# One transformer layer in split fp32 matmuls: both norms of the feed-forward input taken from one variance, and another order of work between attention and feed-forward

## The reference

```python
x = _layernorm(x + attention(x))          # (x - mean) / sqrt(var + 1e-5)
var = jnp.mean(jnp.square(x), axis=-1, keepdims=True)
nx = x * jax.lax.rsqrt(var + 1e-5) * ln_w
x = _layernorm(x + (silu(nx @ gate.T) * (nx @ up.T)) @ down.T)
```

## Time and profile before

| what | value |
|---|---|
| median of 3 runs | 1210.94 us (1209.27 to 1212.98) |
| profiled execution, own time | 1213.92 us |
| its span | 1212.1 us |
| mean granted PE clock | 0.99 |
| PE busy | 1127.9 us, 93% |
| DVE busy | 844.1 us, 70% |
| POOL busy | 780.5 us, 64% |
| ACT busy | 623.9 us, 51% |

### The profile page before, as it was taken

One profiled execution on the slowest core, in us unless ns is written; L12 is line 12 of the kernel. 1 busy time (PEld: TensorE's weight loads), 2 busy tenths in 40 slices (PEclk: granted clock), 3 DMA queues, 4 the chain that ended last, 5 costly groups with the idle time before them and its releaser, 6 DMA issues.

```text
span 1212.1 us, 18710 instructions
## 1 busy us (share of the span) xinstructions
PE 1127.9 (93%) x5346; PEld 943.9 (78%) x5346; DVE 844.1 (70%) x1451; ACT 623.9 (51%) x1138; POOL 780.5 (64%) x511
## 2 busy tenths in 40 slices
PE   7699999999999999999999999999987599999997
PEld 6587878887888788878878887888775478888886
DVE  6688788778877887888788778787888652222224
ACT  4555655555665565656655666566555352222223
POOL 3578867876896688678867886787664123334331
PEclk9999999999999999999999999999999799999999
DMA  6755555555565556565555555555555111111101
GB/s 188 211 136 147 131 135 144 152 133 134 144 159 131 146 144 152 130 153 148 142 136 134 145 136 139 143 143 128 133 134 131 64 53 52 52 52 52 35 17 70
DMA packets 148346, 148.75 MB, mean 123 GB/s; under 512 B 15200, under 2 KB 128864, under 8 KB 148320
## 3 DMA queue, kind: packets, MB, share of 16 engines
q1 hardware_dynamic: 148320, 148.43, 47.8%
HBM read 37.23 MB, written 2.10 MB: 32 GB/s over the span
## 4 chain that ended last, share of the span: by engine, by line
PE 55%; POOL 16%; DVE 13%; issue 9%; ACT 3%; DMA 2%; SPq 1%; DVEq 0%; POOLq 0%; ACTq 0%
PE ACC L1058 11%; PE ACC L1060 11%; PE ACC L1059 11%; POOL rope_s L478 5%; PE S L1058 4%; PE S L1059 4%; PE S L1060 4%; DVE PT_lo L817 4%; POOL qk_raw L481 3%; PE S L1076 3%; PE S L1074 3%; PE S L1075 3%; POOL qk_raw L477 3%; DVE y L869 3%; DVE turned L810 2%
## 5 line engine op out<-in xcount | busy, mean ns | idle before, releaser
L592 ACT ACTIVATE probs<-S,neg_max 128x128 f32<-128x128 f32 (+7 forms) x256 | 189.3, 739 | 276.6 <-DVE neg_max L799 276.6
L799 DVE CUSTOM_DVE_ANT_0 S<-S,mask 128x128 f32<-128x128 f32 (+7 forms) x256 | 194.3, 759 | 152.8 <-PE S L1076 152.3
L810 DVE STREAM_TRANSPOSE turned<-probs 128x128 f32<-128x128 f32 (+7 forms) x256 | 197.8, 773 | 8.3 <-ACT probs L592 8.3
L502 POOL TENSOR_TENSOR PT_lo<-PT_lo,PT_hi 128x512 fp32r<-128x512 f32 x64 | 118.3, 1848 | 123.1 <-ACT PT_hi L599 123.1
L869 DVE SCALAR_TENSOR_TENSOR y<-ACC,row_rcp,y 128x512 f32<-128x512 f32 x256 | 178.4, 735 | 17.1 <-PE ACC L1060 17.0
L599 ACT ACTIVATE PT_hi<-PT_lo 128x1024 fp32r<-128x1024 f32 (+3 forms) x160 | 164.8, 1030 | 12.7 <-DMA PT_lo<-turned 12.3
L1058 PE MATMUL ACC<-PT_hi,V_hi 128*128 128x512 f32 (+3 forms) x384 | 136.4, 355 | 35.2 <-DVE PT_lo L817 20.5
L817 DVE TENSOR_TENSOR PT_lo<-PT_lo,PT_hi 128x1536 fp32r<-128x1536 f32 (+2 forms) x96 | 158.7, 1654 | 4.1 <-ACT PT_hi L599 4.1
L478 POOL TENSOR_TENSOR rope_s<-rope_s,sin_sb 128x512 f32<-128x512 f32 x76 | 146.1, 1922 | 0.0
L481 POOL TENSOR_TENSOR qk_raw<-qk_raw,rope_s 128x512 f32<-128x512 f32 x76 | 134.0, 1763 | 6.0
L1074 PE MATMUL S<-K_hi,Q_hi 128*128 (+5 forms) x384 | 132.0, 344 | 4.6 <-ACT probs L592 3.8
(11 more groups left out here) (130 smaller groups left out, 2589.3 us busy)
## 6 DMA issues: line engine op xcount, KB each, us to landing
PT_lo<-turned SPq DMA_DIRECT2D x256, 128.0 KB, 2.6
PT_lo<-turned SPq DMA_DIRECT2D x128, 208.0 KB, 3.7
rope_s<-qk_raw SPq DMA_DIRECT2D x160, 128.0 KB, 2.8
PT_lo<-turned SPq DMA_DIRECT2D x128, 112.0 KB, 2.5
PT_lo<-turned SPq DMA_DIRECT2D x128, 96.0 KB, 2.4
wq_raw<-in_L_attn_wq_dram SPq DMA_DIRECT2D x32, 256.0 KB, 2.9
wkvo_raw<-in_L_attn_wo_dram SPq DMA_DIRECT2D x32, 256.0 KB, 2.7
turned<-in_L_ffn_gate_w_t_dram SPq DMA_DIRECT2D x7, 512.0 KB, 3.9
```

Of the source, the lines that this page charges most:

```text
L592: nc.scalar.activation(dst, src, ACT.Exp, bias=neg_max[:, at:at + 1], scale=-1.0, accum_out=row_sum[:, j % 2, i:i + 1]).then_inc(exp_done, 1)
L799: nc.vector.tensor_tensor_reduce(src, src, bias, scale=1.0, scalar=MASKED, op0=ALU.add, op1=ALU.min, accum_out=neg_max[:, at:at + 1]).then ...
L810: nc.vector.transpose(dst.rearrange("p b (r i) -> p r b i", i=QB), src.rearrange("p (r b i) -> p r b i", b=4, i=QB)).then_inc(turn_done, 1)
```

## The change

1. **Norms.** The RMS norm's divisor is computed from the layer norm's variance: sqrt(v (1 + 1e-5) + 1e-10), beside sqrt(v + 1e-5). `deviations` makes both with two small square roots, one DVE reciprocal inverts both (128x2x4), and `both_norm` makes `nx` from the un-normalised `y` with one subtraction and multiplication. The eight squares, their row sums and the second turn of square root and reciprocal are gone. `layer_norm` of the residual stays, and now comes after `both_norm`.
2. **Statistics.** `add_with_statistics` puts each `bn_stats` behind the next tile's addition.
3. **Low parts.** For the last head the low parts of pieces 2 and 3 are made by POOL; DVE keeps piece 4. On POOL the first gate and up low parts follow them.
4. **Order.** PE makes `transpose_rows(0)` right after pv of half 1, ahead of `rows` of tiles 4 to 7. On ACT the high parts of the gate and up weights move ahead of the high parts of pieces 3 and 4. On DVE `xT_low(0)` moves ahead of additions 6 and 7.

```diff
-                deviation(cols, mean_var[:, cols, 1], eps_ln, 1.0)
...
-            def rms_deviation(half):
-                for t in range(half * HT, (half + 1) * HT):
-                    act_e.wait_ge(ln_done, t + 1)
-                    if t >= 2:
-                        act_e.wait_ge(sq_done, t - 1)
-                    nc.scalar.activation(V_stage[:, t % 2 * HID:(t % 2 + 1) * HID], y[:, t, :], ACT.Square,
-                                         accum_out=sum_sq[:, t:t + 1]).then_inc(sq_done, 1)
-                act_e.wait_ge(sq_done, (half + 1) * HT)
-                cols = slice(half * HT, (half + 1) * HT)
-                deviation(cols, sum_sq[:, cols], eps_rms, 1.0 / HID)
+                deviation(0, cols, mean_var[:, cols, 1], eps_ln, 1.0)
+                deviation(1, cols, mean_var[:, cols, 1], eps_rms, 1.0 + RMS_EPS)
...
+            n.add("pt1", 3 * (HEADS - 1) - n["pt1"])
+            for k in (2, 3):
+                pt_low(k)
             weight_low(0, gate_raw, gT)
             weight_low(1, up_raw, uT)
...
+            weight_high(0, 0)
+            weight_high(0, 1)
             pt_high(3, HEADS - 1)
             pt_high(4, HEADS - 1)
-            layer_deviation(0)
+            deviations(0)
             split_high("pv", 1)
-            rms_deviation(0)
-            weight_high(0, 0)
-            weight_high(0, 1)
             act_e.wait_ge(ln_w_in, 16)
             xT_high(0, 0, xbank[0], scale=True)
-            layer_deviation(1)
-            rms_deviation(1)
+            deviations(1)
...
+            def add_with_statistics(ts):
+
+                for t in ts:
+                    add_rows(t, REP - 1)
+                    if t > ts[0]:
+                        statistics(t - 1, n["y"] - 1)
+                statistics(ts[-1], n["y"])
+
             splits(*LAST_STEPS[-1], last=True)
+            add_with_statistics(tiles[0])
+            for t in tiles[0]:
+                aggregate(t)
+            n.add("pt1", 2)
+            pt_low(4)
+            inverses(0)
+            for t in tiles[0]:
+                both_norm(t)
+            split_low("pv", 1, REP - 1)
+            for t in tiles[0]:
+                layer_norm(t).then_inc(ln_done, 1)
+            add_with_statistics((4, 5))
             dve.wait_ge(ln_w_in, 16)
...
+            xT_low(0)
+            add_with_statistics((6, 7))
...
             other("pv", 1, REP - 1, 0, NT)
+            transpose_rows(0)
             for t in range(HT, NT):
                 rows(t)
             y_base = n["y"]
-            transpose_rows(0)
```

More of the change, by code:

```diff
@@ L700, in _, with deviation, deviations @@
                 step(j, i, 0, last=True)
-            def deviation(cols, squares, eps, scale):
-                nc.scalar.activation(spread[:, cols], squares, ACT.Sqrt, bias=eps[:], scale=scale).then_inc(std_done, 1)
-            def layer_deviation(half):
+            def deviation(row, cols, squares, eps, scale):
+                nc.scalar.activation(spread[:, row, cols], squares, ACT.Sqrt, bias=eps[:], scale=scale).then_inc(std_done, 1)
+            def deviations(half):
                 act_e.wait_ge(var_done, (half + 1) * HT)
                 cols = slice(half * HT, (half + 1) * HT)
-                deviation(cols, mean_var[:, cols, 1], eps_ln, 1.0)
-            def rms_deviation(half):
-                for t in range(half * HT, (half + 1) * HT):
-                    act_e.wait_ge(ln_done, t + 1)
-                    if t >= 2:
-                        act_e.wait_ge(sq_done, t - 1)
-                    nc.scalar.activation(V_stage[:, t % 2 * HID:(t % 2 + 1) * HID], y[:, t, :], ACT.Square,
-                                         accum_out=sum_sq[:, t:t + 1]).then_inc(sq_done, 1)
-                act_e.wait_ge(sq_done, (half + 1) * HT)
-                cols = slice(half * HT, (half + 1) * HT)
-                deviation(cols, sum_sq[:, cols], eps_rms, 1.0 / HID)
+                deviation(0, cols, mean_var[:, cols, 1], eps_ln, 1.0)
+                deviation(1, cols, mean_var[:, cols, 1], eps_rms, 1.0 + RMS_EPS)
             def weight_high(p, which):
@@ L946, in aggregate, with inverses, norm, both_norm @@
                 nc.vector.bn_aggr(mean_var[:, t, :], stats[:, t, :]).then_inc(var_done, 1)
[L948 to L957, removed]
+            def inverses(half):
+                cols = slice(half * HT, (half + 1) * HT)
+                dve.wait_ge(std_done, 2 * half + 2)
+                nc.vector.reciprocal(inv_spread[:, :, cols], spread[:, :, cols]).then_inc(inv_done, 1)
+                dve.wait_ge(inv_done, half + 1)
+            def norm(dst, t, row):
+                return nc.vector.tensor_scalar(dst, y[:, t, :], mean_var[:, t, 0:1], inv_spread[:, row, t:t + 1],
+                                               ALU.subtract, ALU.mult)
             def layer_norm(t):
[L960 to L965, removed]
+                return norm(y[:, t, :], t, 0)
+            def both_norm(t):
+                norm(nx[t], t, 1).then_inc(nx_done, 1)
             def xT_low(half):
@@ L976, in _ @@
             tiles = [range(HT), range(HT, NT)]
-            cols = [slice(0, HT), slice(HT, NT)]
-            splits(*LAST_STEPS[-1], last=True)
-            dve.wait_ge(ln_w_in, 16)
[L980 to L996, removed]
-            y_base = n["y"]
-            xT_low(0)
-            variances(tiles[1], y_base)
-            inverses(3, cols[1])
+            def add_with_statistics(ts):
[4 more added lines that the diff above has]
+                statistics(ts[-1], n["y"])
+            splits(*LAST_STEPS[-1], last=True)
+            add_with_statistics(tiles[0])
[10 more added lines that the diff above has]
+            add_with_statistics((4, 5))
+            dve.wait_ge(ln_w_in, 16)
+            xT_low(0)
+            add_with_statistics((6, 7))
+            y_base = n["y"]
+            for t in tiles[1]:
+                aggregate(t)
+            inverses(1)
+            for t in tiles[1]:
+                both_norm(t)
             for t in tiles[1]:
                 layer_norm(t).then_inc(ln_done, 1)
-            inverses(4, cols[1])
-            for t in tiles[1]:
-                rms_norm(t)
             product(0, 0, first=True)
```

24 lines of the change are left out of this document (12 added, 12 removed).

## The result

| | before | changed |
|---|---|---|
| median | 1211.53 us (1209.27 to 1212.98, 4 runs) | 1201.8 us (1201.03 to 1202.41, 4 runs) |
| profiled execution, own time | 1213.92 us | 1201.28 us |
| its span | 1212.1 us | 1199.5 us |

The ratio is 0.9921, with a 95% interval of 0.9903 to 0.9939: 9.7 us less. Two more comparisons on other chips gave 0.9919 (0.989 to 0.9947) and 0.9915 (0.9901 to 0.9928). Forecast were 8.45 us less than before, 1202.5 us, in a range of 1198.5 to 1206.5.

The account below looks back on a forecast made before the run. PE was taken as the pace, idle 14 us and partly at a low clock between attention and feed-forward. Gains of 1.95 + 5.1 + 1.4 = 8.45 us gave 1202.5 us, range 1198.5 to 1206.5 (8 in 10).

Parts of the forecast that it names:

- Term 1, start of pv: Before pv of half 1: with two low parts on POOL, PE starts at 950.95 instead of 952.89, gain 1.95 us.
- The letter of the Trainium skill: At DVE's last low part: POOL holds the ports to its end, DVE starts at 949.85, gain 1.75 us.
- The table load: On ACT before piece 3: two weight copies of 1.05 us each fit behind the load, with 0.1 us to spare.
- The rival from the Trainium skill: After ACT's table load: a 1.38 us drain makes copies 0.6 us later, whole gain 7.8 us; chance 0.02.
- pv itself: The pv matmuls of half 1: length stays 7.30 us, 12 matmuls of it at clock 0.50.
- The rival of a fast pv: pv starts at 2.4 GHz, twelve matmuls save 2.4 us: gain 10.85, 1200.1 us; chance 0.15.
- Term 2: From pv's end to gate_up: 7.0 us instead of 12.07, gain 5.1 us.
- Term 3, the clock: First gate_up matmuls: PE stays at 2.4 GHz after shorter pauses, gain 1.4 us, low end 0.
- What had to stay hidden: DVE's norms ahead of transpose_rows(1): done at 972.8, transposes start at 974.8, 2 us to spare.

Follow-up runs that it names:

- the last version: Changed kernel with early layer norms and POOL waiting for them, plus PE's rows 6 and 7 behind the first gate_up unit, xT_low(0) right behind O_lo: ratio 0.9897.
- the kernel with the squares back: Changed kernel's order, but with the squares, their root and the two-step norms of before: ratio 0.9905 to the kernel before, stage 33.24 us.

## Why the prediction was right

The sum was made term by term against the profiled execution; the stage went from 43.30 to 32.87 us, 10.43, where 8.45 were forecast. The mechanism was right. That the forecast median of 1202.5 us lies only 0.7 from the measured 1201.8 is partly luck: the medians moved by 9.7 us, the stage of the profiled executions by 2 us more than forecast.

- **Term 1, start of pv**: forecast 1.95, measured 2.82 in the first execution, 2.39 and 2.97 in the others. The steps held: pieces 2 and 3 took POOL 3.48 and 2.09 us (3.6 and 2.2 estimated from shorter ones), DVE came second and waited, and went ahead of POOL's up weights. The difference is mostly when piece 3 comes. By rows 5 its high part starts 4.3 us after the table load and POOL follows at 5.3; in the three executions POOL started on it at 4.5, 4.9 and 4.3. Over all profiles in which POOL makes this piece it lies between 4.3 and 5.9 us, and it differs between executions of one code (4.3 to 4.9 in the changed kernel), so 0.4 to 1.0 us of this term is luck. A second piece of luck went unseen: the kernel before had run its four `rows` tiles at the low level, so that DVE reached its low parts 8.9 us after the load. With the same order of statistics, at the high level, it was 7.8. About 1 us of this gain is that, in the forecast and in the measurement alike. DVE was let in later than forecast: at 946.5, 0.1 us before POOL's recorded end at 946.64, not 0.2. The letter of the Trainium skill (SBUF — State Buffer, "Who interferes with whom"), by which the first keeps the ports to its end, and the forecast are about equally far off. In all seven executions in which DVE's last low part waited the lead was 0.1 us.
- **The table load**: in the changed kernel the next activation again starts at once, and the copies fit. No drain behind the load shows: the load starts at 937.78 and takes 1.28 us, and the next activation starts at 939.08. The rival from the Trainium skill (ScalarE: Activation LUTs, "What ACT_TABLE_LOAD costs"), with a drain of 1.38 us, falls.
- **pv itself**: 7.30 kept, measured 6.60, 7.37 and 7.53 in the three executions and 6.2 to 7.7 over all kernels here. It starts at the low level in every kernel but the last version, where it started at a granted clock of 1.00 and fell to the low level 1.1 us later; its length varies by 1.5 us. The rival of a fast pv did not come.
- **Term 2**: forecast 5.1, measured 5.52, alike in all three executions. I had added durations end to end; consecutive rows of DVE overlap by some 0.08 us in the records, and there are five such seams. The forecast names one blocked `rms_norm`; two were blocked, and the four took 5.87 us, where they take 1.67 unblocked in the kernel with the squares back. So up to 4.2 of the 5.5 us are POOL's block moved off this stretch, and not arithmetic that is gone.
- **Term 3, the clock**: forecast 1.4, measured 1.39. With pauses of 0.89 and 0.87 us the granted clock stays at 1.00, the 2.4 GHz level.
- **What had to stay hidden**: the last of the norms for tiles 4 to 7 ended at 968.4, 2.3 us before `transpose_rows(1)`; 2 us were forecast.

What the prediction did not see is how the gain divides. It credits the vanished squares and second root with a part of term 2. The experiments show that this edit alone gives nothing (1.0013), and that the changed order without it gives all (0.9905). In the stage, undoing the transposes' place costs 2.3 us behind pv, the weight copies 3.4 to 4.7, the low parts 0.4 to 1.6, the statistics nothing. The place of `xT_low(0)` ahead of additions 6 and 7 was undone only together with the rest.

Not settled is why PE's low level in the four `rows` tiles comes in some executions and not in others, what moves the landing of piece 3, and what moves attention's end by up to 6 us between executions of the same code.

## What to carry to other kernels

When two engines exclude each other, the place of the long instruction on the engine off the path can matter more than its length: 4.8 us of POOL work cost 0.9 to 1.5 us before pv, 4 us after it, and nothing once it waited for the norms. A chain of operations that was shortened gained nothing here while the order stayed as it was; look first for the engine's idle time (3.54 us on DVE before `O_lo`) and move work there. And in a bundle of edits, leave each out in turn as well as trying it alone: the exact scale, first in the title, showed no gain in time either way.

## What was not expected of the hardware

A DVE `TENSOR_TENSOR` of 1.19 us that is let in late delays POOL's next instruction by 1 us: it takes 3.35 us in the changed kernel, 2.37 where nothing stood in the way. The two engines hand over near instruction ends: DVE's low part got in 0.1 us before POOL's recorded end, a norm 0.2 to 0.3. They took turns: in the six executions in which DVE's last low part waited with another POOL instruction queued, it went before that one. Of the norms, one got through between POOL's two instructions.
